# Dual attention on one core: a new order of steps, the last batch's x1 and FD in other buffers, slabs converted in pairs

## The reference

```python
h = group_norm(x, gn_w, gn_b)                       # 32 groups
q, k, v = (conv1x1(h, w, b) for w, b in ((wq, bq), (wk, bk), (wv, bv)))
w = softmax(einsum('bcq,bck->bqk', q, k) / 16)
x1 = x + conv1x1(einsum('bqk,bck->bcq', w, v), wo, bo)

att = einsum('bcn,bdn->bcd', x1, x1)                # channel attention
feat_e = einsum('bcd,bdn->bcn', softmax(max(att) - att), x1)
fb, fc, fd = conv1x1(x1, wb, bb), conv1x1(x1, wc, bc), conv1x1(x1, wd, bd)
att_s = softmax(einsum('bkn,bkm->bnm', fb, fc))     # position attention
feat_p = einsum('bcm,bnm->bcn', fd, att_s)
out = (beta * feat_e + x1) + (alpha * feat_p + x1)
```

## Time and profile before

| | |
|---|---|
| median of the runs | 496.11 us (493.33 to 499.03) |
| profiled execution | 490.88 us, its span 489.1 us |
| TensorE busy | 437.2 us, 89% of the span |
| VectorE busy | 337.4 us, 69% |
| ScalarE busy | 299.7 us, 61% |
| GpSimd busy | 59.2 us, 12% |
| mean granted clock of TensorE | 0.958 |
| DMA transpositions | 64, 36.52 MB with the other loads of their queue, 39.6% of 16 engines |

### The profile page before, as it was taken

One profiled execution on the slowest core, in us unless ns is written; L12 is line 12 of the kernel. 1 busy time (PEld: TensorE's weight loads), 2 busy tenths in 40 slices (PEclk: granted clock), 3 DMA queues, 4 the chain that ended last, 5 costly groups with the idle time before them and its releaser, 6 DMA issues.

```text
span 489.1 us, 5913 instructions
## 1 busy us (share of the span) xinstructions
PE 437.2 (89%) x2078; PEld 360.4 (74%) x2078; DVE 337.4 (69%) x555; ACT 299.7 (61%) x432; POOL 59.2 (12%) x52
## 2 busy tenths in 40 slices
...
GB/s 212 255 1 129 76 94 132 95 79 0 45 95 97 239 85 105 68 88 10 206 129 53 111 139 96 121 0 45 183 120 87 128 122 8 1 160 98 106 67 43
DMA packets 140396, 48.03 MB, mean 98 GB/s; under 512 B 135824, under 2 KB 137296, under 8 KB 140368
## 3 DMA queue, kind: packets, MB, share of 16 engines
q1 hardware_dynamic: 136400, 36.52, 39.6%
...
...
## 4 chain that ended last, share of the span: by engine, by line
PE 73%; DVE 7%; issue 5%; POOL 5%; DMA 4%; ACT 4%; SPq 0%; POOLq 0%; ACTq 0%; DVEq 0%
PE sum_ps L731 12%; PE sum_ps L732 11%; PE sum_ps L733 11%; PE score_ps L731 10%; PE score_ps L732 9%; PE score_ps L733 9%; DMA land<-pieces 3%; PE score_ps L843 3%; PE score_ps L873 3%; POOL xn_l L343 2%; DVE pieces L618 2%; POOL x_l L348 2%; DMA x<-in_L_conv_wo_dram 2%; DVE negmax L602 1%; ACT exps L415 1%
## 5 line engine op out<-in xcount | busy, mean ns | idle before, releaser
L415 ACT ACTIVATE exps<-score_ps,negmax 128x1024 f32<-128x1024 f32 x64 | 71.2, 1112 | 65.0 <-DVE negmax L602 41.3
L434 ACT ACTIVATE pt_h<-land 128x512 fp32r<-128x512 f16 x128 | 75.9, 625 | 40.6 <-PE sum_ps L733 25.5
L602 DVE TENSOR_REDUCE negmax<-score_ps 128x1 f32<-128x1024 f32 x64 | 78.0, 1221 | 28.5 <-PE score_ps L733 20.0
L628 DVE TENSOR_SCALAR pt_l<-land 128x512 fp32r<-128x512 f16 x128 | 63.0, 518 | 36.9 <-PE sum_ps L733 29.8
L618 DVE SCALAR_TENSOR_TENSOR pieces<-exps,recip,pieces 128x1024 f16<-128x1024 f32 x64 | 81.8, 1280 | 6.3 <-ACT pieces L424 6.0
L424 ACT ACTIVATE pieces<-exps,recip 128x1024 f16<-128x1024 f32 x64 | 72.9, 1142 | 16.2 <-DMA land<-pieces 10.4
L731 PE MATMUL sum_ps<-pt_h,fd_h 128*128 128x512 f32 x128 | 53.0, 414 | 11.8 <-ACT pt_h L434 11.8
L731 PE MATMUL sum_ps<-pt_h,v_h 128*128 128x512 f32 x128 | 52.0, 406 | 8.0 <-ACT pt_h L434 5.9
L731 PE MATMUL score_ps<-xn_h,g_h 128*128 128x512 f32 x128 | 51.0, 399 | 2.8 <-DVE g_l L516 2.8
L732 PE MATMUL sum_ps<-pt_l,fd_h 128*128 128x512 f32 x128 | 51.9, 405 | 0.0
L733 PE MATMUL sum_ps<-pt_h,fd_l 128*128 128x512 f32 x128 | 51.7, 404 | 0.0
...
(10 more groups left out here) (128 smaller groups left out, 804.9 us busy)
## 6 DMA issues: line engine op xcount, KB each, us to landing
...
land<-pieces SPq DMA_TRANSPOSE x64, 4.4
...
```

The source lines that it names most:

```text
L415: act.activation(exps[:, n % 2, :], score_ps[s][:, :], ACT.Exp, bias=negmax[:, n % RING:n % RING + 1], scale=1.0, accum_out=rowsum[:, n % ...
L434: act.activation(pt_h[:, n % SLABS, :], land[:, k % 2, 0, t, :], ACT.Copy, scale=1.0 / PIECE)\
L602: dve.tensor_reduce(negmax[:, n % RING:n % RING + 1], score_ps[s][:, :], AX.X, ALU.max, negate=True)\
L628: dve.tensor_scalar(pt_l[:, n % SLABS, :], land[:, k % 2, 1, t, :], 1.0 / PIECE, None, ALU.mult)\
```

## The change

1. New `PE_ORDER`, `ACT_ORDER`, `DVE_ORDER`, `POOL_ORDER`. No step is added or left out but the conversions.
2. `cvh` and `cvl` convert two slabs in one instruction (`slab_pair`), 128 x 1024 instead of 128 x 512, and count two. The wait is for the slab two before the pair to be read; PE's steps still take one slab each.
3. In the last batch x1's parts are written to `xn_h`, `xn_l` and FD's to `v_h`, `v_l` (`x1_parts`, `fd_parts`). `x1h.3` waits for S0.3.7 and V.3.1 instead of `x1_read`.
4. The semaphores `landed` exist once for each half of `land`, and which half and which quarter a tile takes follows from the sum it belongs to (`turn_of`), not from its number. SyncE tests for each tile, not for each fourth, that the half is converted. So tiles of two sums may be mixed: S0.2.4 now stands between S2.1.1 and S2.1.2, S0.3.4 between S2.2.1 and S2.2.2.

TensorE's list, old and new:

```diff
-    BG G.0.0 W V.0.0 S0.0.0 MEAN.1 S0.0.1 VAR.1 S0.0.2 V.0.1 S0.0.3 G.0.1 S0.0.4 S0.0.5 S0.0.6 O0.0.0x1 S0.0.7
-    O0.0.0x5 G.1.0 O0.0.0x2 S0.1.0 MEAN.2 S0.1.1 O0.0.1x2 S0.1.2 VAR.2 S0.1.3 O0.0.1x1 G.1.1 O0.0.1x5 V.1.0
-    XT.0.0 V.1.1 XT.0.1 FBC.0 O0.1.0x1 FD.0.0 ATT.0 S2.0.0 FD.0.1 S2.0.1 AT.0 O0.1.0x5 S2.0.2 ET.0 S2.0.3
-    O0.1.0x2 S0.1.4 O2.0.0x1 S0.1.5 O2.0.0x1 S0.1.6 S0.1.7 O2.0.0x5 S2.0.4 O2.0.0x1 S2.0.5 O2.0.0x1 S2.0.6
-    O2.0.0x1 S2.0.7 G.2.0 O0.1.1x3 MEAN.3 O0.1.1x3 S0.2.0 VAR.3 S0.2.1 O0.1.1x1 S0.2.2 O0.1.1x1 S0.2.3 XT.1.0
-    O2.0.1x2 G.2.1 XT.1.1 V.2.0 O2.0.1x2 FBC.1 ATT.1 V.2.1 AT.1 O2.0.1x3 S2.1.0 O2.0.1x1 S2.1.1 ET.1 O2.0.1x2
-    S2.1.2 S2.1.3 FD.1.0 O0.2.0x3 FD.1.1 O0.2.0x2 S0.2.4 O0.2.0x1 S0.2.5 O0.2.0x1 S0.2.6 O0.2.0x1 S0.2.7
-    O2.1.0x5 G.3.0 O2.1.0x2 S2.1.4 O2.1.0x1 S2.1.5 O2.1.0x1 S2.1.6 O2.1.0x1 S2.1.7 O0.2.1x5 S0.3.0 O0.2.1x1
-    S0.3.1 O0.2.1x1 S0.3.2 O0.2.1x1 S0.3.3 V.3.0 G.3.1 O2.1.1x1 XT.2.0 V.3.1 XT.2.1 O2.1.1x2 ATT.2 O2.1.1x1 AT.2
-    O2.1.1x1 FBC.2 O2.1.1x1 ET.2 O2.1.1x3 S2.2.0 O2.1.1x1 S2.2.1 FD.2.0 S2.2.2 O0.3.0x2 S2.2.3 O0.3.0x1 FD.2.1
-    O0.3.0x2 S0.3.4 O0.3.0x1 S0.3.5 O0.3.0x1 S0.3.6 O0.3.0x1 S0.3.7 O2.2.0x7 S2.2.4 O2.2.0x1 S2.2.5 O2.2.0x1
-    S2.2.6 O2.2.0x1 S2.2.7 O0.3.1x8 O2.2.1x1 XT.3.0 O2.2.1x1 XT.3.1 ATT.3 FBC.3 AT.3 O2.2.1x4 S2.3.0 O2.2.1x1
-    S2.3.1 ET.3 O2.2.1x2 S2.3.2 O2.2.1x1 S2.3.3 FD.3.0 S2.3.4 O2.3.0x2 S2.3.5 FD.3.1 S2.3.6 S2.3.7 O2.3.0x8
-    O2.3.1x10
+    BG G.0.0 W V.0.0 S0.0.0 MEAN.1 S0.0.1 S0.0.2 VAR.1 S0.0.3 G.0.1 V.0.1 S0.0.4 S0.0.5 S0.0.6 S0.0.7 O0.0.0x6
+    G.1.0 O0.0.0x2 S0.1.0 S0.1.1 S0.1.2 S0.1.3 MEAN.2 O0.0.1x2 VAR.2 O0.0.1x6 V.1.0 XT.0.0 V.1.1 XT.0.1 FBC.0
+    G.1.1 ATT.0 O0.1.0x1 S2.0.0 S2.0.1 FD.0.0 O0.1.0x3 AT.0 S2.0.2 S2.0.3 O0.1.0x2 S0.1.4 FD.0.1 S0.1.5 O0.1.0x2
+    S0.1.6 ET.0 S0.1.7 O2.0.0x2 S2.0.4 O2.0.0x1 S2.0.5 O2.0.0x5 S2.0.6 G.2.0 S2.0.7 O2.0.0x2 S0.2.0 S0.2.1
+    O0.1.1x3 S0.2.2 O0.1.1x5 S0.2.3 O2.0.1x3 XT.1.0 O2.0.1x1 G.2.1 O2.0.1x1 FBC.1 O2.0.1x2 XT.1.1 O2.0.1x1 V.2.0
+    S2.1.0 O2.0.1x1 V.2.1 O2.0.1x1 S2.1.1 S0.2.4 ATT.1 O0.2.0x1 S2.1.2 S2.1.3 O0.2.0x2 FD.1.0 AT.1 O0.2.0x1
+    FD.1.1 MEAN.3 S0.2.5 O0.2.0x1 S0.2.6 O0.2.0x1 VAR.3 O0.2.0x2 ET.1 S0.2.7 O2.1.0x6 S2.1.4 S2.1.5 G.3.0
+    O2.1.0x3 S2.1.6 S0.3.0 S2.1.7 O2.1.0x1 S0.3.1 O0.2.1x8 S0.3.2 O2.1.1x2 S0.3.3 V.3.0 O2.1.1x2 FBC.2 O2.1.1x2
+    XT.2.0 O2.1.1x3 XT.2.1 S2.2.0 G.3.1 O2.1.1x1 S2.2.1 V.3.1 ATT.2 S0.3.4 AT.2 S2.2.2 O0.3.0x3 S2.2.3 O0.3.0x1
+    S0.3.5 O0.3.0x2 S0.3.6 FD.2.0 O0.3.0x1 ET.2 O0.3.0x1 S0.3.7 FD.2.1 O2.2.0x3 S2.2.4 O2.2.0x3 S2.2.5 O2.2.0x4
+    S2.2.6 S2.2.7 O0.3.1x8 O2.2.1x2 XT.3.0 FBC.3 O2.2.1x1 XT.3.1 O2.2.1x2 S2.3.0 S2.3.1 O2.2.1x1 S2.3.2 ATT.3
+    AT.3 S2.3.3 S2.3.4 S2.3.5 O2.2.1x1 FD.3.0 S2.3.6 O2.2.1x2 S2.3.7 ET.3 O2.2.1x1 FD.3.1 O2.3.0x10 O2.3.1x10
```

The other two long lists from the last sum of block 0 on. ScalarE, old, then new:

```diff
-    cvh.93 a0.3.6 cvh.94 cvh.95 a0.3.7 exp2.2.4 exp2.2.5 a2.2.4 exp2.2.6 cvh.96 cvh.97 cvh.98 cvh.99 cvh.100
-    a2.2.5 cvh.101 a2.2.6 cvh.102 cvh.103 exp2.2.7 a2.2.7 hXT.3.0 x1h.3.0 hXT.3.1 x1h.3.1 base.3.0 cvh.104
-    cvh.105 cvh.106 cvh.107 base.3.1 cA.3 hFBC.3 cvh.108 expE.3 cvh.109 cvh.110 cvh.111 exp2.3.0 hET.3 exp2.3.1
-    a2.3.0 a2.3.1 exp2.3.2 hFD.3.0 exp2.3.3 a2.3.2 exp2.3.4 a2.3.3 hFD.3.1 exp2.3.5 a2.3.4 exp2.3.6 cvh.112
-    cvh.113 cvh.114 cvh.115 cvh.116 a2.3.5 cvh.117 a2.3.6 cvh.118 cvh.119 exp2.3.7 a2.3.7 cvh.120 cvh.121
...
+    exp0.3.7 a0.3.7 cvh.92 exp2.2.4 cvh.94 a2.2.4 exp2.2.5 cvh.96 cvh.98 a2.2.5 exp2.2.6 cvh.100 exp2.2.7
+    cvh.102 a2.2.6 a2.2.7 x1h.3.0 x1h.3.1 hXT.3.0 cvh.104 cvh.106 hFBC.3 hXT.3.1 cvh.108 base.3.0 base.3.1
+    exp2.3.0 cvh.110 exp2.3.1 a2.3.0 a2.3.1 cA.3 exp2.3.2 exp2.3.3 a2.3.2 exp2.3.4 a2.3.3 hFD.3.0 expE.3
+    exp2.3.5 a2.3.4 hET.3 exp2.3.6 cvh.112 cvh.114 a2.3.5 hFD.3.1 a2.3.6 exp2.3.7 cvh.116 a2.3.7 cvh.118 cvh.120
```

VectorE, new (old: lXT.3.0 lXT.3.1 and four cvl ahead of sA.3, lFBC.3 behind minE.3, b2.3.5 behind cvl.116 and cvl.117):

```diff
+    max2.2.7 cvl.100 b2.2.5 r2.2.6 cvl.102 r2.2.7 b2.2.6 fx.3.1.0 fx.3.1.1 b2.2.7 lXT.3.0 cvl.104 cvl.106 lFBC.3
+    lXT.3.1 max2.3.0 max2.3.1 max2.3.2 r2.3.0 cvl.108 r2.3.1 cvl.110 b2.3.0 b2.3.1 sA.3 aA.3 max2.3.3 r2.3.2
+    max2.3.4 max2.3.5 b2.3.2 r2.3.3 minE.3 r2.3.4 max2.3.6 b2.3.3 lFD.3.0 nE.3 r2.3.5 b2.3.4 lET.3 fo.2.1.0
+    fo.2.1.1 cvl.112 cvl.114 max2.3.7 r2.3.6 b2.3.5 lFD.3.1 b2.3.6 r2.3.7 cvl.116 b2.3.7 cvl.118 fo.3.0.0
```

GpSimd's list and the code (VectorE's `slab_pair` is like ScalarE's; wherever `x1_h`, `x1_l`, `fd_h`, `fd_l` stood, `x1_parts(b)` and `fd_parts(b)` stand):

```diff
-    ldxin.1 rstd.1 xnl.1.0 xnl.1.1 ldxin.2 rstd.2 x1l.0.1 x1l.0.0 xnl.2.0 xnl.2.1 ldxin.3 st.0.0.1 st.0.0.0
-    rstd.3 x1l.1.0 x1l.1.1 st.0.1.0 st.0.1.1 xnl.3.0 xnl.3.1 st.1.0.1 st.1.0.0 x1l.2.1 x1l.2.0 st.1.1.1 st.1.1.0
+    ldxin.1 rstd.1 xnl.1.0 xnl.1.1 ldxin.2 rstd.2 x1l.0.0 x1l.0.1 xnl.2.0 xnl.2.1 ldxin.3 st.0.0.1 st.0.0.0
+    x1l.1.0 x1l.1.1 st.0.1.1 st.0.1.0 rstd.3 xnl.3.0 xnl.3.1 st.1.0.1 st.1.0.0 x1l.2.0 x1l.2.1 st.1.1.1 st.1.1.0
...
+        def x1_parts(b):
+            return (xn_h, xn_l) if b == BATCH - 1 else (x1_h, x1_l)
+        def fd_parts(b):
+            return (v_h, v_l) if b == BATCH - 1 else (fd_h, fd_l)
...
+        landed = [several(f"landed_{half}", QT) for half in range(2)]
...
+        def turn_of(use):
+            name, (b, j) = numbers(use)
+            return SUM[f"O{name[1]}.{b}.{j // QT}"], j % QT
...
-            for n in range(len(TILE)):
-                k, j = divmod(n, QT)
-                if j == 0 and k >= 2:
+            for use, n in TILE.items():
+                k, j = turn_of(use)
+                if k >= 2:
                     sp.wait_ge(slab_high, (k - 1) * NT)
                     sp.wait_ge(slab_low, (k - 1) * NT)
                 sp.wait_ge(both_pieces, n + 1)
                 sp.dma_start_transpose(
                     land[:, k % 2, :, :, cols(j)].rearrange("p a t q -> p (a t) q"),
-                    pieces[:, n % 2, :, :].rearrange("p a n -> p (a n)")).then_inc(landed[j], 16)
+                    pieces[:, n % 2, :, :].rearrange("p a n -> p (a n)")).then_inc(landed[k % 2][j], 16)
...
-                    act.wait_ge(landed[(n - 2) % QT], 16 * ((n - 2) // QT + 1))
+                    k, j = turn_of(TILES[n - 2])
+                    act.wait_ge(landed[k % 2][j], 16 * (k // 2 + 1))
...
-            def slab(n):
+            def slab_pair(n):
                 k, t = divmod(n, NT)
                 if t == 0:
                     for j in range(QT):
-                        act.wait_ge(landed[j], 16 * (k + 1))
+                        act.wait_ge(landed[k % 2][j], 16 * (k // 2 + 1))
                 if n >= SLABS:
-                    act.wait_ge(slab_read, n - SLABS + 1)
-                act.activation(pt_h[:, n % SLABS, :], land[:, k % 2, 0, t, :], ACT.Copy, scale=1.0 / PIECE)\
-                    .then_inc(slab_high, 1)
+                    act.wait_ge(slab_read, n - SLABS + 2)
+                at = n % SLABS
+                act.activation(pt_h[:, at:at + 2, :], land[:, k % 2, 0, t:t + 2, :], ACT.Copy, scale=1.0 / PIECE)\
+                    .then_inc(slab_high, 2)
...
                 elif name == "x1h":
                     b, m = n
                     act.wait_ge(sum_done[m], sum_of(0, b, 1) + 1)
-                    if b:
+                    if b == BATCH - 1:
+                        for use in (f"S0.{b}.7", f"V.{b}.1"):
+                            full(use)
+                    elif b:
                         act.wait_ge(x1_read, b)
-                    high(x1_h[:, m, :], x1s[b % 2][:, m, :]).then_inc(x1_high, 1)
+                    high(x1_parts(b)[0][:, m, :], x1s[b % 2][:, m, :]).then_inc(x1_high, 1)
...
             def sum_steps(use, block_no, b, c):
                 k = SUM[use]
-                v = v_p if block_no == 0 else fd_p
+                v = v_p if block_no == 0 else fd_parts(b)
```

More of the change, by code:

```diff
@@ L35 @@
 """.split()
 ACT_ORDER = """
[L38 to L52, removed]
```

107 lines of the change are left out of this document (56 added, 51 removed).

## The result

The changed kernel takes **454.22 us** (median of 4 runs, 452.23 to 455.11), the kernel before 494.81 (493.33 to 499.03, 4 runs): ratio 0.916, 95% interval 0.909 to 0.923. Forecast were 463 us (450 to 484) and faster; both hold. The profiled execution took 454.26 us, its span is 452.3.

What follows compares the result with a forecast made beforehand. Order of steps and the two-buffer pieces ring bound the kernel, not throughput. Terms -5, -9, -8 and -11 make -33: span 456 us, execution 458, plus 5.2 to the median, 463 us; range 450 to 484.

Steps and rivals of the forecast that it cites:

- 52 us of idleness and low clock: TensorE's idleness and clock losses together from 42 us on; a list without a stall would end at 437 us.
- All that the walks give (42 us): Whole kernel: the gain with nothing kept back for slips, for a time of 454 us.
- The first stage, -5: 42 to 80 us: V.0.1 behind G.0.1 and S0.1 tiles earlier; S0.1.0 starts 5.9 us earlier, 5 taken.
- the walk: All stages: stepping through the new lists with mean durations, 5 us per landing and TensorE at the high clock.
- The middle, -9 and -8: 140 to 183 us: 9 of 10.2 taken; 183 to 398 us: 8 taken, idleness and clock being 11.
- S0.2.4's late transposition: 183 to 398 us: 4.9 us late, moving S2.1.3's high piece by 1.3, 7 us before a sum needs it.
- The last stage, -11: From O0.3.1's end: S2.3.0 7 us earlier, last matmul at 71.5 against 85.5 us; 11 taken, 3 left for clock and slips.
- the ring and DVE's row: Last stage: the two pieces buffers' turn and VectorE's steps per tile set the tiles' pace, 4.3 us a tile.
- The pairs, nothing: Conversions on ACT and DVE: neither engine is the bound, so nothing booked; upper end of the gain 16 us.
- The third rival: All sums: pairs starve TensorE, 0.75 us a wait, 48 over all 64 pairs, 511 us, slower; chance 0.06.
- VectorE's locked conversions: DVE's conversions stretch beside GpSimd subtractions: six times 2.2 us, 13 us of DVE time; 31 with all 14 full-width subtractions.
- The clock's rival, 0.09: Last stage: the low clock level takes 8 us more where no idleness absorbs it, 471 us; chance 0.09.

Runs made afterwards that it cites:

- e10: Changed kernel with the last batch's two low-part subtractions x1l.3.0 and x1l.3.1 on VectorE instead of GpSimd: 450.32 us, ratio 0.914.
- e2: Kernel before's lists up to the end of O0.3.1, new lists and xn/v buffers behind it, single slabs: 483.39 us, ratio 0.978.
- e3: New lists up to the end of O0.3.1, lists and buffers of the kernel before behind it, single slabs: 466.51 us, ratio 0.945.
- e7: New lists to O0.0.0's last step, the kernel before's lists behind it, single slabs, old buffers: 493.69 us, ratio 1.000.
- e9: Changed kernel with a third pieces buffer for the last stage's eight tiles S2.3.n: 452.50 us, ratio 0.917.
- e1: Changed kernel with slabs converted one at a time as before: 453.43 us, ratio 0.916.
- e5: Kernel before, its lists and buffers kept, with slabs converted in pairs: 500.11 us, ratio 1.012.
- e6: Kernel before, its lists and single slabs kept, with the last batch's x1 and FD in xn's and v's buffers: 495.15 us, ratio 1.002.
- e4: Changed kernel with x1's parts and FD of the last batch in their own buffers as before: 456.14 us, ratio 0.923.
- e8: New lists to O2.0.0's last step, the kernel before's lists behind it, single slabs, old buffers: 482.34 us, ratio 0.976.

## Why the prediction was right

**What bounds, and the floor.** Of the 52 us of idleness and low clock named, 37 went in the profiled execution. With the head at the high level it is 42: e10's head with after's middle and end gives E at 48.29 + 322.01 + 71.67 = 442.0, 41.7 before the old one. "All that the walks give (42 us)" was the right size, though the terms as stated (5.9, 10.2, 11 and 14) add up to 41.1. That the order decides and not throughput is shown by e2 and e3: the same instructions in another order, and in e2 into other buffers, gain 40 us.

**The first stage, -5.** With the head at the high level S0.0.4 starts at 45.2 and S0.1.0 at 70.2 to 70.3 (e7, e10), the walk's numbers; in the profiled execution of after 50.2 and 75.2, by the head's clock. So this term gave -1 there and -6 otherwise. It isn't a gain by itself: e7 shows that without the new middle it is paid back.

**The middle, -9 and -8.** From O0.0.0's end to T it is 22.0 us, not 17 (A to T has 1.8 of the first stage's gain besides). No slab wait is left in it, and 0.6 us of idleness; I had kept 4 of the walk's 21 back for slips, and none came. The walk was right to 1 us, which is as well as the old middle is known, and the margin was the error. S0.2.4's late transposition is there, and hidden as reckoned: it is issued at 230.68, 5.5 us after its low piece's end and right behind slab 54's conversion, and TensorE has no wait by it; S0.3.4's is issued 0.1 us after. The longest landing, 9.1 us where 7.2 was the most, is another one's: S2.2.0's, issued at 318.41, beside two loads of x that ScalarE issued at 318.5 and 318.9. The forecast had put these loads at no cost, and TensorE has no wait by this one either.

**The last stage, -11.** It gave 13.8 (the other traces of the old last stage would make it 11.8 to 14.3), the walk 14. In us after T, predicted and then measured: FBC.3 6.1, 6.7; S2.3.0 15.3, 15.7; first low piece's end 23.4, 23.8; eighth 53.4, 53.0; O2.3.1's slabs 60.4, 60.6; last matmul 71.5, 71.7. One step had a reason too many behind a right number: I put the tiles' pace, 4.3 us (4.2 measured), on "the ring and DVE's row", and e9 takes the ring out. What is left is the row, perhaps with the two `exps` buffers. And the buffers of x1, which I gave no price of their own, are 5.2 of the 13.8: 2.6 of waiting and the low level that follows it.

**The pairs, nothing.** 1060 and 692 ns against 1053 and 0.7 to 0.8 estimated. With the new lists they are worth 0.5 us up to T, 0.1 behind it and nothing that a median shows (e3, e2, e1). With the old ones they cost 5 to 6 us (e5), against the "nothing" booked. The third rival's mechanism, a wait inside a sum, is real, but shows once, at 1.3 us; more of the cost is the later first slab, which the prediction had at 0.4 us each (0.4 to 0.8 against e6), and the low level behind the waits.

**VectorE's locked conversions.** Three of 64 pairs took 2.58 to 2.90 us, each beside a full-width subtraction on GpSimd (the one from 191.97 beside two that ran from 189.49 to 194.31), and three more 1.19 to 1.44. In all 8.4 us of VectorE went beyond the median (64 at a mean of 0.824 less 64 at 0.692); I had 13. None held TensorE. The Trainium skill, GPSIMD Engine Reference, section 1 (Specifications), has the two share SBUF interfaces; the trace agrees for the pair too. GpSimd pays as well: x1l.3.0, which started beside a low piece on VectorE, took 2.94 us, against 2.41 on average before. The two subtractions took 2.35 us together on VectorE (e10).

**The clock's rival, 0.09.** It did not come: 1.00 in the last stage with 9.0 us of idleness in it, the longest piece 2.45 us. The Trainium skill, TensorE: Matmul & The Clock Gate, section on HAM oscillation, lets gaps between groups lower the clock; the trace agrees in e4 and e7, behind 5.07 and 2.71 us. But the length of a gap didn't settle it here: behind 2.85 us ahead of slab 24 the level was high in before and e6 and low in e2 and e7, and behind 2.2 us ahead of AT.2 high in before and e2 and low in e6, e7 and e8. Behind the 2.45 us it was high in all three traces that have them (after, e2, e9). So the chance of 0.09 had luck on its side that no run here can size.

**The size of the error**, 463 against 454: 5 in the middle and 2.8 in the last stage too little, 4 in the first too much, and 5.2 for the step from the profiled execution to the median. Before had such a step (5.2 us by the median then known, 3.9 by that of four runs), but it was not to be carried over: the profiled execution of before had its head at the high level, that of after had the low one in itself (454.26, median 454.22). 5.0 + 2.8 - 4.0 + 5.2 = 9.0.
